# A four-layer graph network: first strips split before other loads, matmuls term by term, and 36 fill matmuls at the start of six passes

## What is computed

```python
x = _layernorm(x + L0(x))   # twice: relu(segment_sum(h[col], row) / deg), h = x @ W.T + b; then a linear layer
x = _layernorm(x + L1(x))   # segment_sum(edge_weight * x[src], dst), then two dense layers
x = _layernorm(x + L2(x))   # four steps, 2 heads: 0.5 * segment_sum(prev[src], dst) / deg + attention(q, k, prev)
x = _layernorm(x + L3(x))   # messages per edge from src, dst and edge_attr, summed by dst, then a GRU cell
```

## Time and profile before

| what | value |
|---|---|
| time, median of 3 runs | 6031.7 us |
| lowest and highest run | 6026.68, 6042.44 us |
| span of the profiled execution | 5325.0 us, 78049 instructions |
| TensorE busy | 4321.5 us (81%), mean granted clock 0.918 |
| GpSimd busy | 3251.7 us (61%) |
| VectorE busy | 2815.1 us (53%) |
| ScalarE busy | 1451.2 us (27%) |
| the six passes together | 2246 us of the span |

### The profile page before, as it was taken

One profiled execution on the slowest core, in us unless ns is written; L12 is line 12 of the kernel. 1 busy time (PEld: TensorE's weight loads), 2 busy tenths in 40 slices (PEclk: granted clock), 3 DMA queues, 4 the chain that ended last, 5 costly groups with the idle time before them and its releaser, 6 DMA issues. The chain is left out here.

```text
span 5325.0 us, 78049 instructions
## 1 busy us (share of the span) xinstructions
PE 4321.5 (81%) x26640; PEld 3018.0 (57%) x26640; DVE 2815.1 (53%) x7430; ACT 1451.2 (27%) x2914; POOL 3251.7 (61%) x3382
## 2 busy tenths in 40 slices
PE   4677866979868787788879997999889767777786
PEld 3444434545535556554446664666555467667775
DVE  6588886755367776535562315221432444455554
ACT  1377850010057664111120102010210122222222
POOL 2766626767767775075516661776177367777774
PEclk6789988989989999699989998999999898999998
DMA  4265559999933344195588887988697465555553
GB/s 145 45 61 80 91 100 194 199 182 187 202 80 101 104 126 109 60 289 159 168 265 271 270 248 250 280 268 253 228 303 241 130 171 144 143 149 146 151 153 82
DMA packets 1261118, 909.00 MB, mean 171 GB/s; under 512 B 446403, under 2 KB 1181934, under 8 KB 1260638
## 3 DMA queue, kind: packets, MB, share of 16 engines
q1 hardware_dynamic: 909866, 519.09, 39.3%
q0 software_dynamic: 102704, 232.38, 16.1%
q10 hardware_dynamic: 248132, 152.25, 9.9%
HBM read 696.10 MB, written 118.89 MB: 153 GB/s over the span
## 5 line engine op out<-in xcount | busy, mean ns | idle before, releaser
L1687 PE MATMUL ps<-adj_d,xs_d 128*128 128x464 bf16 (+1 forms) x4704 | 992.8, 367 | 60.1 <-DVE xs_d L1648 60.1
L3166 POOL DMA_INDIRECT rows_mg<-p_tab,src_idx x784 | 758.3, 967 | 273.4 <-issue 238.1
L1601 POOL DMA_INDIRECT rows_d<-xh_tab,src_idx x632 | 617.7, 977 | 479.8 <-POOLq L187 207.4
L1601 POOL DMA_INDIRECT rows_d<-x_tab,src_idx x512 | 499.1, 975 | 475.5 <-POOLq L187 264.4
L1687 PEld LDWEIGHTS ps<-adj_d,xs_d 128*128 128x128 bf16 x4704 | 466.1, 101 | 509.1 <-DVE xs_d L1648 61.9
L1295 POOL DMA_INDIRECT rows_d<-h_tab,slot_idx x490 | 497.0, 1014 | 266.9 <-issue 143.9
L2216 POOL DMA_INDIRECT rows_g<-x_tab,src_idx x444 | 434.2, 978 | 164.7 <-issue 127.3
L3263 PE MATMUL ps<-win_mg,turned_hot_mg 128*128 128x128 f32 x1568 | 341.2, 302 | 201.2 <-DVE pre_mg L3215 201.0
L1431 PE MATMUL ps<-adj_d,xs_d 128*128 128x512 bf16 (+1 forms) x2028 | 441.0, 375 | 54.6 <-DVE xs_d L1396 49.9
L1673 PEld LDWEIGHTS ps<-onehot_d,rows_d 128*128 128x128 f32 x3552 | 428.6, 192 | 66.6 <-DVE onehot_d L1619 33.5
L1673 PE MATMUL ps<-onehot_d,rows_d 128*128 128x72 f32 (+1 forms) x3552 | 421.4, 275 | 31.3 <-DVE onehot_d L1619 26.3
(11 more groups left out here) (442 smaller groups left out, 7541.4 us busy)
## 6 DMA issues: line engine op xcount, KB each, us to landing
adj_d<-adjacency SPq DMA_DIRECT2D x140, 812.0 KB
adj_d<-adjacency SPq DMA_DIRECT2D x84, 857.5 KB
attr_mg<-in_edge_attr SPq DMA_DIRECT2D x195, 256.0 KB
xp_g<-x_tab SPq DMA_DIRECT2D x70, 448.0 KB
k_rows_d<-k_tab ACTq DMA_DIRECT2D x56, 448.0 KB
loc_mg<-loc_rows SPq DMA_DIRECT2D x196, 128.0 KB
q_s<-q_tab SPq DMA_DIRECT2D x42, 448.0 KB
rden_s<-rden_tab SPq DMA_DIRECT2D x42, 448.0 KB
```

Of the source, the lines that this page charges most:

```text
L1601: nc.gpsimd.indirect_dma_start(rows[:, q % GR * K + k, :], None, table, bass.IndirectOffsetOnAxis(ap=src_idx[:, j:j + 1], axis=0)).then_in ...
L1687: last = nc.tensor.matmul(ps[:, m % 2, 0:w], xs[:, g * GW + k, e, :], adj[:, slot, k, 0:w], start=(g == 0 and k == 0 and e == 0), stop=(g ...
L3166: nc.gpsimd.indirect_dma_start(rows[:, q % RR, k, :], None, p_tab, bass.IndirectOffsetOnAxis(ap=src_idx[:, j:j + 1], axis=0)).then_inc(row ...
```

## The change

It has four parts. (1) `keep_busy` puts 36 float32 matmuls of the identity with a matrix of ones, 128 by 128, into a bank of PSUM that is free, ahead of TensorE's first tile in each of the six passes. (2) ScalarE splits the first strip before it issues the loads of the other works. (3) Within a tile, the matmuls go term by term: all blocks with the high term, then all with the middle, then all with the low one, and where a strip is new, each term is waited for by itself. (4) In dense passes, the pieces are due from tile 3 and no longer from tile 1.

```diff
+FIRST_WAIT = 36
...
+        def keep_busy():
+
+            for k in range(FIRST_WAIT):
+                nc.tensor.matmul(ps[:, 7, 0:P], ident[:, :], ones_mat[:, :], start=True, stop=True)
...
 (source_pass, scalar)
                         for g in range(SPLIT):
                             load(g)
-                        node.start(nc.scalar)
-                        if not count:
-                            act.dma_start(target[:, :], dst_target[:, FAR:TILES]).then_inc(target_in, 16)
                         for t in range(tiles):
                             m, g, c, w = place(t)
                             if m == 0:
                                 split_rows(g)
+                            if t == 0:
+                                node.start(nc.scalar)
+                                if not count:
+                                    act.dma_start(target[:, :], dst_target[:, FAR:TILES]).then_inc(target_in, 16)
 (source_pass, tensor)
+                        keep_busy()
                         for t in range(tiles):
...
-                            if m == 0:
-                                pe.wait_ge(low, g + 1)
...
-                            for k in range(PARTS[g]):
-                                for e in range(TERMS):
+                            for e, term in enumerate((high, middle, low)):
+                                if m == 0:
+                                    pe.wait_ge(term, g + 1)
+                                for k in range(PARTS[g]):
 (dense_pass, table of pieces)
-                        due[1 + k * (tiles - 1) // len(pieces)].append((before, piece))
+                        due[3 + k * (tiles - 3) // len(pieces)].append((before, piece))
 (dense_pass, scalar)
-                        for work in works:
-                            work.start(nc.scalar)
                         for t in range(tiles):
                             m, g = order[t]
                             if splits_at(t) is not None:
                                 split_rows(*splits_at(t))
+                            if t == 0:
+                                for work in works:
+                                    work.start(nc.scalar)
 (dense_pass, tensor)
+                        keep_busy()
                         for t in range(tiles + 1):
...
-                            if m % blocks == 0:
-                                pe.wait_ge(low, h * G + g + 1)
...
-                            for k in range(GW):
-                                for e in range(TERMS):
+                            for e, term in enumerate((high, middle, low)):
+                                if m % blocks == 0:
+                                    pe.wait_ge(term, h * G + g + 1)
+                                for k in range(GW):
```

## The result

The change takes 6077.84 us (median of 4 runs, 6060.88 to 6095.06), the kernel before beside it 6029.19 us: a ratio of 1.0071, with an interval of 1.0045 to 1.0096. The forecast was 6036 us with a range up to 6054; the time lies above it, and the change is slower, by more than the 0.3% that a measurement can tell.

What follows compares the result with a forecast made beforehand. GpSimd's queue was taken to bound passes 00, 01 and 24, TensorE passes 21 to 23. 0 - 8 - 8.5 + 16.3 + 4.4 = +4.2 us on 6031.7 gave 6036 us; 8-in-10 range 6016 to 6054.

Steps and rivals of the forecast that it cites:

- The basis: Whole kernel: the sum is added to the 6031.7 us median, with 706.7 us outside the 5325.0 us span left untouched.
- The table of pieces, gaps: Pass 21's pieces: 49.7 us of TensorE gaps in 21 waits against 33.4 us before, +16.3 us.
- The table of pieces, clock: Pass 21's pieces: seven more gaps at 0.6 us each of lost clock give +4.4 us.
- The start of pass 21: First tile and two pieces of pass 21: full clock and no wait for keys, -8.5 us, between -4 and -10.
- this wait goes: Start of pass 21: TensorE's 3.51 us wait for keys vanishes, as the deferred keys are wanted only at tile 3.
- Passes 22 and 23: Starts of these dense passes: first tile done earlier at full clock, 4 us gained in each, -8 us together.
- Passes 00, 01 and 24: These three passes, bound by GpSimd's queue: 0 us, with bounds of -5 and +3 us.
- fill too long: Pass starts: clock stays at 1.2 GHz through the fill, +4.8 us in each of 22 and 23; 6062 us, chance 0.12.

Runs made afterwards that it cites:

- fill_again: Kernel before with only the fill of 36 matmuls ahead of the six passes, run a second time; ratio 1.0016 to the kernel before.
- table_again: Kernel before with only the pieces dealt out from tile 3 instead of tile 1, run a second time; ratio 1.0071 to the kernel before.
- control: Kernel before, unchanged, profiled again; ratio 0.9985 to the kernel before, pass 21 455.5 us.
- pairs_only: Kernel before with only a new table in pass 21, sums of head 0 sharing a tile with products of head 1; ratio 0.9927 to the kernel before.
- change_pairs: The change with only pass 21's table replaced, sums of head 0 sharing a tile with products of head 1; ratio 0.9927 to the kernel before.
- pairs_wide: Kernel before with terms in turn, pass 21's table pairing sums with the next head's products, and a fill of 9 matmuls of 512 columns; ratio 0.9925.
- fill_narrow: Kernel before with a fill of 36 matmuls of 32 columns; ratio 1.0047 to the kernel before.
- change_again: The change itself, unchanged, run again where the kernel before takes 5320.8 us; ratio 1.0063 to the kernel before.
- fill_wide: Kernel before with a fill of 9 matmuls of 512 columns; ratio 0.9988 to the kernel before.

## Why the prediction was wrong

- **The basis** was wrong first. The 706.7 us "outside the span" do not exist. The old profile is like the executions of the last two comparisons (5321 and 5331 us); the median that I added the sum to came from a chip like the first three. The sign of the result does not hang on this: the change is slower by 0.63% where the trace is like the old one and by 0.71% where it isn't.
- **The table of pieces, gaps** (+16.3 us): right. The idle time of the second half grew by 12.7 us, by 14 waits of 36.0 and 7 of 14.0 us.
- **The table of pieces, clock** (+4.4 us): this step failed, by 16.6 us. I took the clock's loss of the old trace, 8.9 us over 14 gaps, as a fixed price of 0.6 us a gap and multiplied it by seven. Busy time grew by 21.0 us instead: the clock fell 3 times in this part before and 12 times with three gaps in every group. The price of a gap was read from one execution and is not fixed; in fill_again the old gaps by themselves cost 13.1 us more than in the old trace. How much of the 21.0 us the added gaps make, and how much that spread, is open. The two terms together were 20.7 us with an upper bound of 28; measured 34.0.
- **The start of pass 21** (-8.5 us): this step failed as badly, by 18.3 us. The pass is 43.8 us longer in the change and 34.0 with the table alone, so start, fill and split together cost 9.8 us there, 7.3 of them by the end of tile 20. The fill took 10.84 us (10.3 foretold) and the first tile was done 2.9 us earlier after the pass began (15.63 against 18.51), but "this wait goes" was wrong. The 3.51 us of the earlier trace rows were a wait for the second set of keys and `x`, and I reasoned about the deferred first set. The second set's loads are issued when ScalarE does the first piece, 12.23 us after the start of the pass for `x` before and 20.62 in the change, and it is wanted directly behind the first product in both. The wait became 8.95 us. By fill_again (8.97 us with the fill alone) and table_again (0.80 us with the table alone) it comes with the fill, behind which the rows land later.
- **Passes 22 and 23** (-8 us): the first tile was done 3.4 and 2.0 us earlier (14.50 against 17.95, 15.49 against 17.54), by the mechanism that I gave, and the fill took 9.9 us, between my 8.0 and 10.3. Of this, 1.6 us went into a wait for keys in 22, and the passes were 0.0 and 2.1 us shorter. A first tile that is done earlier is no gain by itself. In the forecast's own comparison not even that came: on that kind of chip the first tiles were done 2.6 and 2.4 us later than in the control, with TensorE standing between their matmuls.
- **Passes 00, 01 and 24** (0 us): 321.1, 353.7 and 332.6 us against 324.2, 356.5 and 331.8. The first two are shorter by 3 us, more than the 2 us that I had set as a bound; with the old starts they took 323.6 and 356.4 (pairs_only), and with the terms in turn pass 01 took 367.0 and 367.2 us in change_pairs and pairs_wide, so one profile can't tell this from no change.
- **The rival "fill too long"** (6062 us) came nearest in time by another cause. The fill raised the clock, so its price never came due; only fill_narrow, where the clock stayed low, behaved like it. By the Trainium skill, "TensorE: Matmul & The Clock Gate", Part 4 (PE-mode transpose), a transpose-mode multiplication doesn't count as work for the clock; the fill is not in that mode, and the granted clock rose to 1.00 within it. No run here multiplies in transpose mode, so the rule itself isn't tested.

On the sum: 34.0 (table) + 9.8 (start of 21) - 2.1 (22, 23) - 5.9 (00, 01) + 0.8 (24) = 36.6 us by single profiles, and 5356.51 - 5320.84 = 35.7 us by the medians. That the two agree so well is in part luck: the spans of the two profiles differ by 20.3 us only, since the stages that the change does not touch were together 16.3 us shorter in the second.

What is shown without single profiles is the cause by the medians: the table alone costs 0.71% and 0.90%, and the change with another table of pass 21 loses nothing.

What stays open: why chips differ by 13% for the same program, and why TensorE stands before matmuls that wait for nothing and its signals are late on the slower ones; no run here changes that. There the table costs more (44.8 us in pass 21) and the 36 matmuls of the fill 0.55%, which the traces place only in part.

## What to carry to other kernels

Before a sum is added to a median, check that span and time belong together: a gap of 12% between them means that profile and runs are not of the same kind of execution. Price idle gaps of TensorE with the clock that follows them, and take that price from more than one profile: the same ten gaps went with 10.2 us of low clock in one execution and with 37.5 in another. When an instruction is moved, look at which of several loads TensorE really waited for, and when that one is issued. When work is dealt out by a formula, look at which pieces it makes neighbours: here one line that paired sums with the next head's products was worth 0.73%, and the one that paired products with their own sums cost 0.71%, while three careful edits at the starts were worth nothing.

## What the runs showed of the hardware

- The same program took 5321 to 5331 us on two chips and 6024 to 6070 us on three others. The last stage took 1336.2 us in control and 1043.3 in fill_again, with the same instructions in that stage. Windows of it (columns as above), control, then fill_again:

```profile
4683.00:6019.00 1336.00, 928.77 (x5733) 808.41 (x5733) 498.07 (x1576) 264.65 (x434) 755.23 (x784) 0.79 0.40 111
```

```profile
4302.00:5345.00 1043.00, 780.49 (x5733) 707.87 (x5733) 510.64 (x1576) 262.76 (x434) 757.39 (x784) 0.93 0.53 143
```

VectorE, ScalarE and GpSimd are as busy within 3%. TensorE is busy 148 us longer, at a clock of 0.79 against 0.93, and idle 145 us longer (407 against 262 us). In control, 288 gaps of over 0.2 us, 207.8 us in all, stand in this stage before matmuls that wait for no semaphore; in fill_again none does.
- In control, 57 of the 212 adjacency loads of the four dense passes that wait for an earlier tile are issued over 1 us after that tile's last matmul, up to 13.4 us; in the old trace, change_again, table_again, change_pairs, pairs_only and fill_again none is. In passes 22 and 23 the longest fall on tiles 21, 30, 37, 44, 52 and 60 or 61 in control, and mostly on these or the ones beside them in the change too, although the fill adds instructions ahead of them.
- 36 matmuls of 32 columns kept TensorE busy for 15.54 us, and the granted clock stayed at 0.50 to the end of the fill in all six passes of fill_narrow. With 128 columns (fills of 9.8 to 10.9 us in change_again) and with 512 (9.4 to 10.8 us in fill_wide) it was at 1.00 before the end of each of the six fills.
- Gaps of TensorE of 1.8 to 3.3 us were followed by stretches at the lower clock, but not each time: behind the same ten gaps the clock was low for 10.2 us in one execution and for 37.5 us in another.
